# Making the query projection transposed in a fused cross-attention and mixture-of-experts kernel

## The reference, cut to what matters

```
def _w8a8_linear(x, w, b):
    qx, sx = _dyn_quant(x)       # integers, a scale for each token
    qw, sw = _quant_weight(w)    # integers, a scale for each output channel
    y = jnp.einsum('bnc,oc->bno', qx, qw) * (sx * sw[:, 0])
    return y + b
q = _w8a8_linear(x, wq, bq).reshape(B, N, H, D).transpose(0, 2, 1, 3)
...
scores = jnp.einsum('bhnd,bhld->bhnl', q, k) * inv_sqrt_d + mask[:, None]
attn = jax.nn.softmax(scores, axis=-1)
o = jnp.einsum('bhnl,bhld->bhnd', attn, v)
...
x = x + _L0_ffn_ref(_layernorm(x, axis=-1), ...)
```

## Time and profile before

| | |
|---|---|
| time, median of 3 runs | 1606.87 us (1602.88 to 1607.51) |
| the profiled execution | 1609.71 us, its span 1608.0 us |
| PE busy | 1494.6 us, 93% |
| DVE, ACT, POOL busy | 56%, 55%, 41% |
| mean granted TensorE clock | 0.965 of full speed |

### The profile page before, as it was taken

How to read it: one execution, slowest core, us unless ns; L and a number is a source line. 1 busy time by engine, 2 the same in 40 slices (tenths; PEclk the granted TensorE clock), 3 DMA queues, 4 the chain that set the end, 5 groups by cost and what they waited for, 6 DMA issues and landing times. The chain is left out here.

```text
span 1608.0 us, 40123 instructions
## 1 busy us (share of the span) xinstructions
PE 1494.6 (93%) x11594; PEld 1317.6 (82%) x11595; DVE 897.5 (56%) x2365; ACT 884.0 (55%) x2097; POOL 660.6 (41%) x671
## 2 busy tenths in 40 slices
PE   2899999999999999999999999984399999999896
PEld 2788888888888888888888888873299999999895
DVE  6557666766676667666766676654632222222221
ACT  2467667677777776777677767761033333333232
POOL 4233334333443234323432343323555555656453
PEclk9999999999999999999999999985599999999998
DMA  5567777677767776777677767654537776666643
GB/s 173 145 170 196 209 200 197 179 228 205 194 178 226 202 196 179 225 205 196 178 225 201 200 179 222 185 142 141 160 68 186 182 175 134 148 154 125 160 77 48
DMA packets 220124, 281.09 MB, mean 175 GB/s; under 512 B 83568, under 2 KB 164976, under 8 KB 220080
## 3 DMA queue, kind: packets, MB, share of 16 engines
q1 hardware_dynamic: 203952, 247.24, 54.3%
q0 software_dynamic: 16128, 33.30, 11.6%
HBM read 118.31 MB, written 66.17 MB: 115 GB/s over the span
## 5 line engine op out<-in xcount | busy, mean ns | idle before, releaser
L464 DVE CUSTOM_DVE_ANT_0 probs<-score,neg_mask 112x375 f32<-112x375 f32 x512 | 279.7, 546 | 254.8 <-PE score L555 251.5
L392 ACT ACTIVATE probs<-probs,neg_max 112x375 f32<-112x375 f32 x512 | 312.3, 610 | 197.2 <-DVE neg_max L464 191.7
L563 PE MATMUL turn<-ident,probs 112*125 112x112 f32 x1536 | 264.8, 282 | 2.8 <-ACT probs L392 2.5
L385 ACT ACTIVATE probs_t<-turn 125x336 f32<-125x336 f32 x512 | 226.0, 441 | 71.6 <-PE turn L563 70.6
L563 PEld LDWEIGHTS turn<-ident,probs 112*125 112x125 f32 x1536 | 227.2, 190 | 36.4 <-issue 14.4
L555 PE MATMUL score<-k_stack,q_stack 96*112 96x376 f32 x512 | 209.4, 409 | 8.5 <-DMA q_stack<-q_lo 6.2
L591 PE MATMUL proj<-ctx_hi,wk_hi 128*128 128x376 f32 x512 | 176.0, 344 | 1.9 <-PEq L29 1.1
L591 PE MATMUL proj<-ctx_lo,wk_hi 128*128 128x376 f32 x512 | 172.0, 336 | 0.0
L591 PE MATMUL proj<-ctx_hi,wk_lo 128*128 128x376 f32 x512 | 171.7, 335 | 0.0
L1032 DVE TENSOR_TENSOR a_lo<-a_ps,a_hi 128x384 fp32r<-128x384 f32 x63 | 35.1, 557 | 243.7 <-ACT a_hi L1007 243.7
L596 PE MATMUL proj<-wv_hi,ctx_hi 128*125 128x512 f32 x384 | 151.8, 395 | 0.0
(11 more groups left out here) (198 smaller groups left out, 3393.9 us busy)
## 6 DMA issues: line engine op xcount, KB each, us to landing
k_stack<-k_hi SPq DMA_DIRECT2D x512, 94.0 KB, 2.2
k_stack<-k_lo SPq DMA_DIRECT2D x256, 94.0 KB, 2.2
ctx_stage<-ctx_t SPq DMA_DIRECT2D x32, 750.0 KB, 5.0
q_stack<-q_hi SPq DMA_DIRECT2D x256, 56.0 KB, 2.0
w_raw<-gate_up_t SPq DMA_DIRECT2D x32, 352.0 KB, 3.1
gate_up_dram_hi<-w_hi SPq DMA_DIRECT2D x32, 352.0 KB, 4.8
gate_up_dram_lo<-w_raw SPq DMA_DIRECT2D x32, 352.0 KB, 5.2
gate_up_hi<-gate_up_dram_hi SPq DMA_DIRECT2D x16, 704.0 KB, 4.9
```

What stands on the lines that cost most here:

```text
L385: act.activation(probs_t[:, h % RING_T, :, :], turn[h % 2][0:LC, 0:LT * N].rearrange("p (l n) -> p l n", l=LT), ACT.Copy).then_inc(turned_ ...
L392: act.activation(probs[:, h % DS, :], probs[:, h % DS, :], ACT.Exp, bias=neg_max[:, par % 2, h:h + 1], scale=-1.0, accum_out=total[:, par ...
L464: dve.tensor_tensor_reduce(probs[:, h % DS, :], score[h % 2][0:N, 0:L], neg_mask[:, p, :], 1.0, BIG, ALU.add, ALU.min, neg_max[:, p, h:h + ...
L563: mm = pe.transpose(turn[h % 2][0:LC, l * N:(l + 1) * N], probs[:, h % DS, l * LC:(l + 1) * LC], W["ident"][0:N, 0:N])
```

## The change

The weight blocks `wq_int` become stationary and the tokens `x_int_t` move: 16 matmuls of 128x112 instead of 4 of 112x512, and the result lies with channels on partitions, as the scores need it. The 4 transposes of q and their wait go. Since tokens now lie along the free axis, the token scale is needed as a row on all partitions: SP stores the column `x_scale` to DRAM (`x_scales`), waits for that store, and loads it back as a row for 128 partitions (`x_scale_row`). POOL multiplies it with the column of weight scales into `q_scale`, which DVE uses at head 8. ACT and DVE read `q_t` in SBUF at heads 9 and 10, where they read PSUM. In `prepare_weights` the row of q's weight scales is no longer made (4 transposing matmuls and a copy). 14 semaphore increments are put ahead of DVE's passes.

```diff
@@ SP, attention
                 if has_n:
+                    need(sp, ln1, 8 * n + 5)
+                    with nc.allow_non_contiguous_dma(reason="one scale a token"):
+                        sp.dma_start(x_scales[n, :].rearrange("(p a) -> p a", a=1), x_scale[:, (par + 1) % 2:(par + 1) % 2 + 1]).then_inc(x_scale_stored, 16)
                     need(sp, masked, H * (n - 1))
                     sp.dma_start(neg_mask[:, (par + 1) % 2, :], mask[n, :, :]).then_inc(mask_in, 16)
+                    need(sp, x_scale_stored, 16 * (n + 1))
+                    need(sp, q_scaled, n)
+                    sp.dma_start(x_scale_row[:, :], x_scales[n, :].rearrange("(a t) -> a t", a=1).to_broadcast([128, N])).then_inc(x_scale_in, 16)
@@ POOL
-                    need(pool, q_made, 3 * n)
-                    pool.tensor_tensor(q_tok[:, :], q_tok[:, :], W["bq_row"][0:N, :], ALU.add).then_inc(q_biased, 1)
+                    need(pool, x_scale_in, 16 * (n + 1))
+                    need(pool, q_out, 3 * n)
+                    pool.tensor_tensor(q_scale[:, :, :], x_scale_row[:, :].unsqueeze(1).to_broadcast([128, G4, N]),
+                                       W["wq_col"][:, :].unsqueeze(2).to_broadcast([128, G4, N]), ALU.mult).then_inc(q_scaled, 1)
+                    pool.tensor_tensor(q_t[:, :, :], q_t[:, :, :], W["bq_col"][:, :].unsqueeze(2).to_broadcast([128, G4, N]),
+                                       ALU.add).then_inc(q_biased, 1)
@@ DVE, head 8
-                        dve.scalar_tensor_tensor(q_tok[:, :], misc[0:N, :], x_scale[:, q:q + 1], W["wq_row"][0:N, :],
-                                                 ALU.mult, ALU.mult).then_inc(q_out, 1)
+                        need(dve, q_scaled, n + 1)
+                        dve.tensor_tensor(q_t[:, :, :], misc[:, 0:G4 * N].rearrange("p (g n) -> p g n", g=G4), q_scale[:, :, :],
+                                          ALU.mult).then_inc(q_out, 1)
@@ PE, heads 7 and 9
-                        for t in range(KT):
-                            mm = pe.matmul(misc[0:N, :], x_int_t[:, t, :], W["wq_int"][:, t, :], start=(t == 0), stop=(t == KT - 1))
+                        for g in range(G4):
+                            for t in range(KT):
+                                mm = pe.matmul(misc[:, g * N:(g + 1) * N], W["wq_int"][:, t, 128 * g:128 * g + 128], x_int_t[:, t, :],
+                                               start=(t == 0), stop=(t == KT - 1))
-                    if h == 9 and has_n:
-                        need(pe, q_biased, n + 1)
-                        turn_to_misc(lambda t: q_tok[:, 128 * t:128 * t + 128], W["ident"][0:N, 0:N], misc, N, 128).then_inc(q_made, 1)
```

More of the change, by code:

```diff
@@ L97, in _ @@
             act.wait_ge(ident_made, 3)
-            for i in range(2):
-                act.wait_ge(scale_done, i + 1)
-                for t in range(KT):
-                    act.activation(spread[:, i, t, :], ones[:, :], ACT.Copy, scale=scale[:, i, t:t + 1]).then_inc(spread_done, 1)
+            act.wait_ge(scale_done, 2)
+            for t in range(KT):
+                act.activation(spread[:, t, :], ones[:, :], ACT.Copy, scale=scale[:, 1, t:t + 1]).then_inc(spread_done, 1)
             act.wait_ge(W["ctx_in"], 16)
@@ L104, in _ @@
             act.activation(W["c_hi"][:, 0, :, :], W["stage"][:, :, :], ACT.Identity).then_inc(W["c_hi_made"], 1)
-            for i, (_, _, row) in enumerate(pairs):
-                act.wait_ge(row_made, i + 1)
-                act.activation(row[0:N, :], ps[0:N, :], ACT.Copy, scale=-inv_sqrt_d if i == 0 else 1.0).then_inc(row_out, 1)
+            act.wait_ge(row_made, 1)
+            act.activation(W["wo_row"][0:N, :], ps[0:N, :], ACT.Copy).then_inc(row_out, 1)
         @block.vector
         def _(dve):
-            for i, (n, _, _) in enumerate(pairs):
+            for i, (n, _) in enumerate(pairs):
                 dve.wait_ge(loaded[n], 16)
@@ L128, in _ @@
                                       ALU.subtract).then_inc(ints_done, 1)
-            for i, (_, dst, _) in enumerate(pairs):
+            for i, (_, dst) in enumerate(pairs):
                 for t in range(KT):
@@ L136, in _ @@
             dve.wait_ge(rows_loaded, 16 * 5)
-            dve.tensor_scalar(W["bq_row"][:, :], W["bq_row"][:, :], -inv_sqrt_d, None, ALU.mult).then_inc(bias_done, 1)
+            dve.tensor_scalar(W["bq_col"][:, :], W["bq_col"][:, :], -inv_sqrt_d, None, ALU.mult).then_inc(bias_done, 1)
+            dve.tensor_scalar(W["wq_col"][:, :], scale[:, 0, :], -inv_sqrt_d, None, ALU.mult).then_inc(bias_done, 1)
         @block.tensor
@@ L151, in _, with attention @@
                     mm.then_inc(turned, 1)
[L152 to L161, removed]
+            pe.wait_ge(spread_done, KT)
+            for t in range(KT):
+                mm = pe.matmul(ps[0:N, 128 * t:128 * t + 128], spread[:, t, :], W["ident"][:, :],
+                               start=True, stop=True)
+            mm.then_inc(row_made, 1)
+def attention(nc, W, x, ctx_t, mask, x1, h2, x_scales):
     B, N, C = x.shape
@@ L203, in attention @@
         x_int, x_int_t = sb("x_int", [N, C], BF16), sb("x_int_t", [128, KT, N], BF16)
-        q_tok = sb("q_tok", [N, C])
+        q_t = sb("q_t", [128, G4, N])
+        x_scale_row, q_scale = sb("x_scale_row", [128, N]), sb("q_scale", [128, G4, N])
         out_ts = sb("out_ts", [128, G4, N])
@@ L238, in attention @@
         waits_taken = sem("waits_taken")
+        LOOP_OFFSET = 14
         def need(eng, s, count):
@@ L421, in body @@
                     if h == 9 and has_n:
-                        need(act, q_made, 3 * n + 3)
+                        need(act, q_biased, n + 1)
                         need(act, q_stacked, 16 * QDMAS * n)
-                        act.activation(q_hi[:, :, :], misc[:, 0:G4 * N].rearrange("p (g n) -> p g n", g=G4),
-                                       ACT.Identity).then_inc(q_hi_made, 1)
+                        act.activation(q_hi[:, :, :], q_t[:, :, :], ACT.Identity).then_inc(q_hi_made, 1)
                     if h == 10 and has_nn and (inside or nn > 0):
@@ L540, in body @@
                     if h == 14 and has_nn:
-                        need(dve, q_made, 3 * (nn - 1) + 1)
+                        need(dve, q_made, 2 * (nn - 1) + 1)
                         quantize(x_in[:, p, :], x_amax[:, :], x_scale[:, p:p + 1], x_inv[:, :], x_in[:, p, :], x_int[:, :], ln1, 8 * nn + 4)
+            for _ in range(LOOP_OFFSET):
+                waited(dve)
             iterations(dve, body)
@@ L645, in body @@
                         if has_n:
-                            need(pe, q_out, 3 * n + 3)
+                            need(pe, q_out, 3 * n + 2)
                         if has_m2:
@@ L1135, in program @@
             attention(nc, W, x, ctx_t, mask, out[0:T, :].rearrange("(b n) c -> b n c", n=N),
-                      h2.rearrange("(b n) c -> b n c", n=N))
+                      h2.rearrange("(b n) c -> b n c", n=N), dram("x_scales", (B, N)))
         sb = lambda name, shape, dt=F32: ctx.enter_context(nc.sbuf_tensor(name, shape, dt))
```

21 lines of the change are left out of this document (11 added, 10 removed).

## The result

The changed kernel takes **1826.43 us** (median, 1824.53 to 1830.66) against 1607.12 for the kernel before: ratio 1.1375, 95% interval 1.1347 to 1.1403. The forecast was 1677, range 1642 to 1708. The direction and the place were right; the loss is three times the one forecast.

What follows compares the result with a forecast made beforehand. PE and SP's DMA queue bound the kernel almost equally, with SP setting the changed pass. SP's excess of 69 us, +2 for early passes and -1 for preparation gave +70 on 1609.7; less 2.8 above median, 1677 us, range 1642 to 1708.

Steps and rivals of the forecast that it cites:

- What bounds the changed kernel: SP's in-order DMA queue: 31.57 us occupied plus 1.1 for two issues plus 1.9 wait, 34.6 us a pass.
- such a wait as a sign of being wrong: SP still waiting for PE's scores in the changed kernel would speak against the forecast; no such waits were expected.
- Rival 3: SP is no bound and swallows all 3 us; PE's 0.53 us and preparation remain: 1590 us, chance 0.05.
- the bound on the store's landing from above: Scale store on SP's queue: lands no slower than the mask, 3.4 us, or x1's store, 3.7 us.
- The other end of the detour: Reload and POOL's product make DVE wait 2 to 3 us at head 8 each pass; costed at nothing.
- PE, q's matmuls and transposes: On PE, 16 small matmuls take 0.84 us against 0.87 before; dropping the transposes saves 0.53 us a pass.
- The landing: Scale store to DRAM on SP's queue: lands in 2.9 us, making SP wait 1.9 us a pass.
- 1 (fast landing): Rival: the store lands in 2.0 us, SP stands 1.0 us, pass 33.7 us: 1648 us, chance 0.17.
- 2 (the clock): Rival: PE's 2.8 us gap at head 0 drops the clock, costing 0.5 to 1 us a pass: 1700, chance 0.12.
- 4: Rival: SP absorbs about 2.5 us and the pass stays at 32.3 us: 1605 us, chance 0.04.

Runs made afterwards that it cites:

- e5: Changed kernel, wait kept, the 112 stored words placed 512 bytes apart in DRAM, row loaded from x: 1674 us, 1.0411 to the kernel before.
- e9: e5 without the wait for the store's landing: 1625.5 us, 1.0103 to the kernel before.
- e1: Changed kernel without the store of token scales and its wait, row loaded from x: 1609 us, 1.0028 to the kernel before.
- e6: Changed kernel, wait kept, storing 112 rows of 512 bytes instead of 112 words, row loaded from x: 1676 us, 1.0424 to the kernel before.
- e7: Changed kernel, wait kept, the 112 words copied within SBUF instead of to DRAM, row loaded from x: 1678 us, 1.0435 to the kernel before.
- e2: Changed kernel with the store issued but no wait for it, row loaded from x: 1788 us, 1.1140 to the kernel before.
- e3: Changed kernel with the store issued earlier, ahead of the 12 DMAs of stack_keys(1), computing everything: 1675 us, 1.0430 to the kernel before.
- e11: Changed kernel, wait kept, storing only the first 16 words, next to each other, row loaded from x: 1685 us, 1.0475 to the kernel before.

## Why the prediction was wrong

**What bounds the changed kernel** was right. SP's 31.57 us of occupation plus what is added gives the pass: with the measured wait, 31.57 + 1.1 + 6.3 = 39.0 against 39.29, and SP's remaining wait for scores, 0.3 us a pass, is the rest. In e5 and e9, too, the pass less SP's waits is 32.65 us, for 31.57 + 1.1 forecast. The forecast had no waits for scores at all and named such a wait as a sign of being wrong; 0.3 us a pass were left in the changed kernel and 0.4 in e5. Rival 3 does not follow from them, since the occupation is there in full. Nearer to the old pass the picture of two separate bounds is too simple: in e1 neither queue is full, and each waits for the other.

**The step that failed is the bound on the store's landing from above.** The prediction took 3.4 us (the mask) or 3.7 (x1's store) as its upper end and 2.9 as its value. It was 7.4, and SP stood 6.3 us a pass where the sum has 1.9. Both rows are of transfers with rows of 1500 bytes and more; I took the size of a transfer as what makes it slow, and a tiny one as safe. e5, e6 and e7 show that the rest of that step held: the three stores at this place whose pieces are not neighbours in DRAM give 1674 to 1678, where the forecast had said 1677. That this is so close is in part luck: in e5 SP's wait is 0.4 us a pass shorter than forecast, and its wait for scores, 0.4 us, makes up for it. The error was 4.4 us a pass of SP's wait, and the range could not hold it, because its upper end came from transfers that lack the very property that mattered. A transfer of a kind that no row shows deserved an upper end beyond all rows, not the largest of them.

**The other end of the detour** was costed at nothing, with DVE late by 2 to 3 us and PE's idle time as its cover. The reload was issued 4.4 us later than forecast and took 4.2 us for 2.1, so DVE stood 8.5 us. That is beyond PE's cover, and PE stood 5.0 us a pass for the softmax. In the changed kernel this hid behind SP's wait, since SP's sum gives the whole pass without it: that nothing was priced did no harm to the number, which was luck. e2 shows it as a bound of its own: without SP's wait, the late mask and POOL's order behind it keep the run at 1788. In e5, where the landing is near the forecast, DVE stood 2.2 us a pass and the cover held.

**PE, q's matmuls and transposes:** right, 0.80 us for 0.84, 50 ns each. The Trainium skill, page "TensorE: Matmul & The Clock Gate", section "Back-to-back issue gap", has about 81 ns for such a pair; the trace does not agree, and the row was the better guide. **The landing:** words apart land in 2.5 us and neighbouring words in 7.4. The Trainium skill, page "DMA: Bandwidth & Descriptors", section "Anatomy of one DMA", has a fixed cost of about 2.0 us; it gives it for DMAs issued from GpSimd, and these are SP's. The 2.5 us are near it, the 7.4 us are not.

**Rivals.** 1 (fast landing) fell: even words apart take 2.5 us. 2 (the clock): the clock did fall, to a mean of 0.92 over the loop, but behind the 5.64 us gap at head 11. At the place of the forecast, in front of head 0 in e5, the gaps were 1.6 us on average and 3.4 at most. There, too, the clock fell at times; here is e5 behind a gap of 1.86 us that ended at 473.92:

```profile
476.00:479.00 3.00, 3.00 (x12) 3.00 (x11) 1.04 (x5) 1.59 (x5) 1.27 (x1) 0.50 1.03 332
```

The loop's mean clock stayed at 0.99, and as SP's queue accounts for the whole of e5's pass, no part of the time is left for the clock. So rival 2 had the event, though less often than in every other pass, and not the price. 3 and 4 fell, and rival 3's price of 1590 was too good anyway: e1, with no store and only the reload, is at 1609, since one more DMA on SP, as the waits of e1 show, takes PE's 0.53 us back.

## What to carry to other kernels

A queue that only issues DMAs has an occupation like an engine: take the length of a pass less its waits, and do this before believing a 99% busy engine. Do not turn a column into a row through DRAM with one word per partition to neighbouring addresses; spread the words (64 bytes apart was enough here) or, better, use a matmul against the identity, which here took 0.27 us and no DMA. When an engine does several things in a fixed order, ask which of them its output really waited for: in e2 it was the mask, which has nothing to do with q. Bound an operation that no row shows by more than its nearest rows, and ask which property of it none of them has.

## What the hardware showed that was not expected

A DMA of 112 words of 4 bytes from 112 partitions to neighbouring DRAM addresses lands in 7.4 us. The same words 64 or 512 bytes apart land in 2.5 us, words copied within SBUF and whole rows of 512 bytes in 2.6. The slow one also delays what is issued behind it on the same queue: the mask from 3.4 to 10.7 us and the keys from 2.2 to 5.2 when nobody waits (e2). While it is under way the DMA engines stand still: 0 GB/s from 628 to 630 us in the changed kernel, 8 to 15 GB/s from 609 to 613 us in e2. That the writes to one stretch of memory go one after another is a reading that fits the distance and, roughly, the number; it was argued and not shown, and no run looked inside the memory.

Open: the reload took 4.2 us in the changed kernel and in e3, and 2.9 in e5, which reads x. A freshly written place is not needed for so long a landing: in e1, which reads x and has no store at all, the row takes 4.1 us right behind the mask, and in e9 and e11, which read x too, 3.5. What makes it 4.2 in the changed kernel, where the mask lands as the row is issued, was not separated.
